# Attention over a convolved sequence: a new order of the first step, a second staging buffer for weights, and batches 3 and 4 split a step later

## The reference, cut to what matters

```python
z   = layer_norm_over_channels(x)
g   = group_norm(z, 32 groups) * gamma + beta
qkv = conv1d(g, w_qkv, 16 taps, "same") + b_qkv        # 256 -> 768 channels
a   = softmax(q k / sqrt(64)) v                        # 4 heads of 64 channels
h   = conv1d(a, w_proj, 5 taps) + b_proj
x1  = x + z + h
t   = layer_norm_over_channels(x1)                     # tokens, 256 wide
out = x1 + t + small table work on t (find first marks, shift, add 2 at the digits)
```

## Time and profile before

| | us |
|---|---|
| median of 3 runs | 1193.16 (1191.77 to 1196.22) |
| the profiled execution | 1190.26 |
| its span on the core | 1188.5 |
| TensorE busy | 1016.5 (86%) |
| VectorE busy | 862.2 (73%) |
| ScalarE busy | 575.1 (48%) |
| GpSimd busy | 231.3 (19%) |

### The profile page before, as it was taken

The page is one execution under the profiler, slowest core; times in us unless marked ns, Lnnn a source line. Parts: engine busy times, 40 slices in busy tenths (PEclk is TensorE's granted clock), DMA queues, the critical chain, the costliest instruction groups (busy, mean ns, idle before and its releaser), DMA issues.

```text
span 1188.5 us, 17778 instructions
## 1 busy us (share of the span) xinstructions
PE 1016.5 (86%) x6760; PEld 670.0 (56%) x6760; DVE 862.2 (73%) x1655; ACT 575.1 (48%) x794; POOL 231.3 (19%) x164
## 2 busy tenths in 40 slices
PE   2737395999999999997989899999999998988854
PEld 1425262666566655664655466656666666756644
DVE  7985976767576578786868566667658675988867
ACT  3443343545445445645547355544435455555522
POOL 2541724100000113112121100000010003223221
PEclk9859697999999999998989899999999999999987
DMA  4240105375275435651654157426533763434412
GB/s 147 80 180 25 45 28 214 74 159 93 50 164 112 80 71 127 145 85 36 195 120 77 36 122 146 89 54 156 95 71 72 191 127 87 107 60 100 107 54 71
DMA packets 279775, 120.44 MB, mean 101 GB/s; under 512 B 267665, under 2 KB 270097, under 8 KB 276753
## 3 DMA queue, kind: packets, MB, share of 16 engines
q1 hardware_dynamic: 279696, 119.37, 43.5%
HBM read 37.43 MB, written 14.81 MB: 44 GB/s over the span
## 4 chain that ended last, share of the span: by engine, by line
PE 45%; DVE 31%; issue 9%; DMA 6%; ACT 5%; POOL 3%; SPq 1%; DVEq 0%; ACTq 0%; POOLq 0%
PE cP L838 11%; PE cM L838 10%; PE cQ L838 8%; PE psV L905 8%; DVE arena L1218 4%; DVE smx L1228 4%; DMA arena<-arena 3%; PE psS L865 3%; PE psT L865 3%; DMA H<-w_qkv 2%; DVE W L1012 2%; DVE W L1005 2%; POOL wsum L466 2%; ACT arena L709 1%; DVE arena L1026 1%
## 5 line engine op out<-in xcount | busy, mean ns | idle before, releaser
L838 PE MATMUL cM<-U,W 128*128 128x256 f16 (+1 forms) x1536 | 230.3, 307 | 47.8 <-ACT m_sb L693 17.8
L838 PE MATMUL cP<-U,W 128*128 128x256 f16 (+1 forms) x1536 | 227.5, 305 | 17.0 <-DVE yqk L1066 11.9
L709 ACT ACTIVATE arena<-arena,smx 128x1024 f16<-128x1024 f32 x128 | 146.8, 1147 | 173.2 <-DVE smx L1261 170.9
L838 PE MATMUL cQ<-U,W 128*128 128x256 f16 (+1 forms) x1536 | 220.6, 300 | 0.0
L838 PEld LDWEIGHTS cM<-U,W 128*128 128x128 f16 x1536 | 152.4, 99 | 120.4 <-ACT m_sb L693 18.1
L838 PEld LDWEIGHTS cP<-U,W 128*128 128x128 f16 x1536 | 151.6, 99 | 84.9 <-DVE yqk L1066 12.2
L838 PEld LDWEIGHTS cQ<-U,W 128*128 128x128 f16 x1536 | 149.2, 97 | 65.1 <-issue 1.6
L1218 DVE SCALAR_TENSOR_TENSOR arena<-arena,smx 128x1024 f16<-128x1024 f32 x128 | 167.6, 1309 | 20.0 <-ACT arena L709 19.9
L905 PE MATMUL psV<-arena 128*128 128x512 f16 x512 | 124.0, 398 | 37.4 <-DMA arena<-arena 37.4
L1270 DVE SCALAR_TENSOR_TENSOR arena<-psV,arena 64x512 f32<-64x512 f32 x32 | 22.0, 689 | 152.0 <-ACT arena L716 151.9
L687 ACT ACTIVATE arena<-psS,smx,esc 128x1024 f32<-128x1024 f32 x64 | 76.9, 1202 | 75.1 <-DVE smx L1229 75.1
(11 more groups left out here) (196 smaller groups left out, 1235.6 us busy)
## 6 DMA issues: line engine op xcount, KB each, us to landing
U<-kept_u SPq DMA_DIRECT2D x6, 2077.0 KB, 9.9
H<-w_qkv SPq DMA_DIRECT2D x12, 1024.0 KB, 7.6
kept_u<-U SPq DMA_DIRECT2D x2, 2077.0 KB, 10.3
kept_u<-arena SPq DMA_DIRECT2D x2, 2077.0 KB, 6.9
arena<-x_tok SPq DMA_DIRECT2D x8, 512.0 KB, 9.0
W<-x_tok SPq DMA_DIRECT2D x4, 1024.0 KB, 6.1
out_tok<-W SPq DMA_DIRECT2D x3, 1024.0 KB, 4.3
kept_h<-arena SPq DMA_DIRECT2D x4, 514.0 KB, 4.5
```

Source lines behind the costliest of these rows:

```text
L709: a(phl[:, i % 3, 0, :], prob[:, i % 2, :], ACT.Copy, scale=smx[:, i % 2, 4:5]) \
L838: last = mm(out, W[:, j, wl, c, wat + tap, :], U[:, slot, ul, c, at:at + width], start=(c == 0 and tap == 0 and wl + ul == 0), stop=(c == ...
```

## The change

It has seven parts.

1. **A second staging buffer.** Tile 1's weights go to `wst_b` at the arena's end, all others to `wst_a` in a new tensor `staging`, which also holds H1 later. Tile 1's load needs no wait. Loads come in four quarters, in steps 2 and 3 one behind each of four transposes.
2. **Scales from squares.** In place of VectorE's two maxima per tile (L987) ScalarE squares the staged weights, 2048 elements a partition, with a sum read-out (kind `wmax`); VectorE adds the two sums (`wtop`), and `pow2(..., squared=True)` takes a power of two from the root.
3. **A new order of step 0** and of steps 3 and 4 in `EXTRA` and `START`; all extra work now stands at the end of its slot on every engine, and TensorE's `weight_top` comes behind the slot's matmuls.
4. **Batches 2 and 3 (the third and fourth) are split a step later**, in steps 1 and 2, from `eo` kept in memory (`keep_eo`, `load_eo`) and straight into `U`; `aside` is gone. VectorE now makes batch 1's differences too.
5. **VectorE's slot**: the row constant right after the y work and ahead of the q/k low parts.
6. **The key copies** (L1092, L1093) become a DMA between partitions (`copy_k`).
7. **Heads a slot later**, at 6, 10, 14 and at slot 0 of the next step. The loops over steps 1, 2 and 5, 6 are written out.

```diff
+        wst_b = arena[:, edge[-1] - WST:edge[-1]].rearrange("p (c s k o) -> p c s k o", c=CT, s=2, k=PH_TAPS)
+        staging = sb("staging", [P, 2 * EO], F32)
+        H1 = staging[:, 0:NB * HR // 2].bitcast(F16).rearrange("p (l b r w) -> p l b r w", l=2, b=NB, r=2)
+        wst_a = staging[:, 0:WST].rearrange("p (c s k o) -> p c s k o", c=CT, s=2, k=PH_TAPS)
+        eo_b = staging[:, 0:EO].rearrange("p (c r w) -> p c r w", c=CT, r=2)
...
-        def pow2(ch, src, k, scale, inverse):
+        def pow2(ch, src, k, scale, inverse, squared=False):
             v = nc.vector
             ch.step(v.tensor_scalar(inverse, src, 1e-30, None, ALU.max))
-            ch.step(v.tensor_scalar(bits[:, 0:1], inverse.bitcast(I32), 0x7F800000, None, ALU.bitwise_and))
+            if squared:
+                k -= 64
+                ch.step(v.tensor_scalar(bits[:, 0:1], inverse.bitcast(I32), 1, 0x7F800000, ALU.logical_shift_right,
+                                        ALU.bitwise_and))
+            else:
+                ch.step(v.tensor_scalar(bits[:, 0:1], inverse.bitcast(I32), 0x7F800000, None, ALU.bitwise_and))
...
-        WSTAGES = ("wmax0", "wmax1", "wscale", "wsum0", "wsum1", "wsum2", "w00", "w01", "wsum3", "w10", "w11")
+        WSTAGES = ("wmax", "wtop", "wscale", "wsum0", "wsum1", "wsum2", "w00", "w01", "wsum3", "w10", "w11")
...
         EXTRA = {
-            0: table(batch_input(1, 0, 4, 4, 7, 7, 7, 10), tile_weights(1, (1, 1, 2, 2, 2, 2, 2, 2, 2, 2, 2)),
-                     batch_input(2, 6, 10, 10, 13, 13, 13, 14), tile_weights(2, (8, 8, 9, 9, 9, 9, 9, 9, 9, 9, 9)),
-                     batch_input(3, 13, 16, 15, 17, 17, 17, 17), [(4, ("wtop", 1)), (10, ("wtop", 2)), (17, ("ring", 0))]),
-            3: table(tile_weights(3, (1, 3, 4, 4, 5, 6, 8, 8, 9, 10, 10)), tile_weights(4, (12, 14, 15, 15, 16, 17, 17)),
-                     [(4, ("wtop", 3)), (15, ("wtop", 4))]),
-            4: table(list(zip((1, 3, 4, 5), [(kind, 4) for kind in WSTAGES[7:]])),
-                     tile_weights(5, (7, 8, 9, 9, 10, 11, 11, 12, 12, 14, 15)),
-                     [(9, ("wtop", 5)), (16, ("pads", 0))]),
+            0: table(tile_weights(1, 1, 1, 2, 3, 3, 4, 5, 5, 6, 6, 7), batch_input(1, 2, 5, 5, 7, 7, 7),
+                     batch_split(1, 8, 9, 9), tile_weights(2, 8, 8, 9, 10, 10, 11, 12, 12, 13, 13, 14),
+                     batch_input(2, 6, 9, 9, 11, 11, 11), batch_input(3, 12, 14, 14, 16, 16, 16)),
+            1: table(batch_split(2, 3, 5, 7), [(1, ("ring", 0))]),
+            2: table(batch_split(3, 3, 5, 7)),
+            3: table(tile_weights(3, 6, 6, 7, 7, 8, 8, 9, 10, 10, 11, 12), tile_weights(4, 15, 15, 16, 16, 17)),
+            4: table(tile_weights(4, no, no, no, no, no, 1, 1, 2, 3, 4, 5),
+                     tile_weights(5, 8, 8, 9, 9, 10, 10, 11, 11, 12, 13, 14), [(16, ("pads", 0))]),
...
+        START = {"vector": ("ln", "gstat", "wscale", "gn", "wsum0", "first0", "wsum1", "first1", "split0", "wsum2", "split1",
+                            "w00", "w01", "split2", "wsum3", "w10", "w11"),
+                 "scalar": ("ln", "wmax", "wsum0", "gn", "first0", "wsum1", "first1", "phase", "split0", "wsum2", "split1",
+                            "w00", "w01", "split2", "wsum3", "w10", "w11"),
+                 "gpsimd": ("wsum0", "wsum1", "split0", "wsum2", "split1", "split2", "wsum3")}
...
+            def copy_k(k, hd):
+                sp.wait_ge(S["qk_lo"], 2 * (2 * k + hd + 1))
+                sp.dma_start(stack[0:D, hd, 1:3, :].rearrange("p k t -> p (k t)"),
+                             stack[D:P, hd, 1:3, :].rearrange("p k t -> p (k t)")).then_inc(S["qk_done"], 16)
...
                     turn(k, u)
+                    if u == 3:
+                        copy_k(k, 1)
+                    if k == 0 and u == 9:
+                        load_eo(3)
+                        keep_u(2)
+                    if k == 1 and u == 9:
+                        keep_u(3)
+                    if k == 1 and 12 <= u < 16:
+                        if u == 12:
+                            sp.wait_ge(S["ulo_done"], SPLITS * NB)
+                        load_w(3, [u - 12])
+                    if 2 <= k < STEPS - 2 and 4 <= u < 8:
+                        load_u(k + 2, u - 4)
+                    if k == 2 and 11 <= u < 15:
+                        load_w(4, [u - 11])
+                    if k == 3 and u in (5, 6):
+                        load_w(5, [2 * u - 10, 2 * u - 9])
+                    if u == 14 and k < STEPS - 1:
+                        copy_k(k + 1, 0)
...
+                if kind == "wmax":
+                    wait(act, "wam_done", k)
+                    if k >= 3:
+                        act.wait_ge(S["conv_done"], GROUPS * (3 * TILES + j + 1))
+                    for c in range(CT):
+                        weights_in(act, k, c)
+                        a(W[:, j, 0, c, 0:2 * PH_TAPS], wst(k)[:, c].rearrange("p s k o -> p (s k) o"), ACT.Square,
+                          accum_out=am[:, 4 + c:5 + c]).then_inc(S["c_m"], 1)
```

More of the change, by code:

```diff
@@ L532, in add_common @@
                     .then_inc(S["ya_done"], 1)
-            def step(n, more=None):
+            for n in range(STEPS):
                 for i in range(SLOTS):
-                    for entry in EXTRA.get(more, {}).get(i, []):
-                        extra(*entry)
                     if i in (3, 9, 16):
@@ L825, in conv_item @@
                 if (g, c, t) == (0, 1, 0):
[L826 removed]
+                    if n == 0 and j == 0:
                         pe.wait_ge(S["ulo_done"], 1)
@@ L1275, in step @@
+                    if attn and i in (6, 10, 14):
+                        heads(k, i // 4 - 1)
+                    if not conv and i == 17:
+                        heads(k, 3)
+                    for entry in EXTRA.get(n, {}).get(i, []):
+                        extra(*entry)
                     if not conv:
```

446 lines of the change are left out of this document (210 added, 236 removed).

## The result

The changed kernel took **1240.81 us** (median, 1239.1 to 1241.99) beside 1193.81 for the kernel before on the same chip: ratio 1.0392 [1.0368, 1.0416], so 47 us slower where 37 faster was forecast. The profiled execution's span is 1239.9 us, 51.4 more than before.

What follows compares the result with a forecast made beforehand. Quiet steps were taken as TensorE-bound near 108 us, with gains only above that and the last step VectorE's; -10 - 11 - 6 + 1 + 0 - 11 = -37 gave a median of 1156 us, own range 1144 to 1168.

Steps and rivals of the forecast that it cites:

- step 0: First step: maxima become squares, splits move out, order changes; -10 us, bounds -20 and +3, value transposes near 177.
- step 1: Second step: batch 3's split leaves its first 12 us, later splits hide in VectorE's slack; -11 us, bounds -13 and -5.
- steps 3 and 4: Steps making the second half's weights: about 30 us above quiet steps against 38 now, taken as 0, bounds -15 and +15.
- last step: Attention and projection: key copies gone and fewer VectorE waits for products; -11 us, bounds -3 and -17.
- Rival (d): Weight tops in steps 3 and 4: split loads make each of three wait 15 us more; +45, 1201 us; chance 0.04.
- sign of being wrong: Whole kernel: TensorE's waits for tops past 70 us, a table load beside a square, or late transposes in steps 2 to 4.
- Rival (a): Waits only change names: step 0 ends where it did, steps 3 and 4 grow by 10; 1176 us; chance 0.2.
- The end of every step: Last unit: earlier reciprocal and key-copy DMA save 3 us, more than TensorE's 1.64 wait; steps 2, 5, 6, 7 give -6.
- What hides them is that slack: Steps 1 and 2: splits, about 6 us of VectorE each, hide in its 37 us free per step.
- Rival (c): Squares on ScalarE: Square needs another table, three tops pay two loads each, 7.7 us; 1164 us; chance 0.04.
- Gone, 9.2 less: Last step: two key copies of 4.62 us under GpSimd's additions vanish; 6 kept, as the next low half pays.
- It is VectorE's: Last step: VectorE bounds it, busy 148.9 of 186.0 us, so removing its copies and waits should give -11.

Runs made afterwards that it cites:

- extra ahead alone: Changed kernel with extra work, from step 1 on, at the slot's head on ScalarE and GpSimd and behind VectorE's low half: 1211.92 us, ratio 1.0158.
- fastest version: Changed kernel with heads, weights of tiles 3 to 5 and extra work (from step 1) placed as before, splits in slots 4, 5, 5: 1163.78 us.
- splits in other slots: Changed kernel with the splits of batches 2 and 3 in slots 4, 5, 5 in place of 3, 5, 7: 1230.43 us, ratio 1.0322.
- heads back: Changed kernel with the heads' output in slots 5, 9, 13 and 17 again, as before the change: 1219.97 us, ratio 1.0236.
- old order of weights: Changed kernel with tiles 3 to 5 in their former slots, VectorE's maxima, and whole loads for tiles 4 and 5: 1224.62 us, ratio 1.0256.

## Why the prediction was wrong, point by point

| part | forecast | measured |
|---|---|---|
| step 0 | -10 | -7.3 |
| step 1 | -11 | -1.3 |
| step 2 | -0.5 | +13.0 |
| steps 3 and 4 | 0 | +40.9 |
| steps 5 to 7 | -4.5 | +1.4 |
| last step | -11 | +4.8 |
| sum | -37 | +51.4 (terms rounded) |

**Steps 3 and 4 are where it failed, and the step that failed is the one not taken.** The text reckoned 30 us above two quiet steps, for the tops' stalls, two slots packed with sums and the slow clock behind them, against 38 in the kernel before, and took 0 as the difference. Measured are 79 above two quiet steps. The change lists that all extra work moves to the end of its slot, and the sum gave that edit no term. Alone it is worth 28.9 us (extra ahead alone), and it is not a matter of busy time: ScalarE's part used to fill the time in which it waits for the maximum, and VectorE's the time in which it waits for the exponential. Put last on both engines, the two halves of one weights tile follow one another and stand between two units. The tops, which were costed, came out at 6.90, 11.22 and 9.72 against 7.6, 4 to 7 and 5 to 7.5. The middle one had its last quarter load late by 3.93 us and the two squares behind it; while VectorE waited for them (7.72 us) the low half of its unit waited too. Rival (d), the only one that made the kernel slower, wanted 15 us more at each top. They came out at most 4.2 above the reckoning, and whole loads with old slots gave 16.2 us, not 45. The text's own sign of being wrong, waits for tops past 70 us in all, did not fire either: they were 66.1 in a kernel 47 us slower. Rival (a) had the direction, steps 3 and 4 longer, but with 10 us and for the tops alone.

**The end of every step: the mechanism was right, the sum was eaten.** "The reciprocal stands ahead of the q/k remainder and the copies go to a DMA": in the kernel before those two edits brought the quiet steps to 107.4, to a tenth what was forecast. Steps 2, 5, 6 and 7 gained 8.6 where 6 was forecast, and steps 3 and 4 another 12 where the text had none, 22 us in all in the medians. The text read the 37.4 us of the earlier trace rows as the last product of a step; by the timeline 16.6 of them lie in the last step and 11.4 in steps 3 and 4, and only the 1.64 of step 2 was carried to the other quiet steps. In the changed kernel the heads took much of it back. The text moved "heads a slot later" only in the last step and kept 5 us for it as a gain; in the other steps it stands just ahead of the last unit of a group, and the move costs 20.8.

**Step 1 and step 2.** "What hides them is that slack" was wrong. VectorE has 37 us free in a step, but the splits stand in the in-order chain of a unit. The value transposes of step 1, forecast near 287, came at 300.7. Even in the fastest version steps 1 and 2 take 117.4 and 114.3, together 231.7 against 231.3 before: spreading two splits over two steps moved 5 us from one to the other and gained nothing there. Their slots in the changed kernel add 8.8 in these steps on top (splits in other slots).

**Step 0** stands: both long tops and the value transposes came within 3 us of the walk (58, 116 and 180), and the 17.8 us stall is gone. How much of the 7.3 is the second buffer, the order or the split moved out isn't shown: no run takes them apart. VectorE lost 31.5 us of work there (145.99 to 114.54) for a step 7.3 shorter. The squares are at the lower end of the estimate of 4.2 to 4.5, by the groups by line and shape of the changed kernel:

```profile
L663 ACT ACTIVATE W<-staging 128x2048 f16<-128x2048 f32 x10 | 19.0, 1903 | 7.1 <-DMA staging<-w_qkv 7.1
...
L663 ACT ACTIVATION_READ_ACCUMULATOR W<-staging 128x1 f32 x10 | 1.9, 193 | 0.0
```

A pair is 4.2 by these means and 3.9 in the timeline of tile 1's (53.73 to 57.60). Rival (c) is refuted: the table loads of the changed kernel stand on L605 (three) and L742 (two), none on L663, by the same view. (Its sentence "none around copies" misread the kernel before, where two more loads stand on L678, the copies of the values.)

**The last step.** "Gone, 9.2 less" took the copies' 4.62 us as their own. GpSimd's two additions, in the kernel before (timeline; the second copy is in the earlier trace rows):

```profile
1033.75 4.89 POOL L508 TENSOR_TENSOR W<-W 128x2048 f32<-128x2048 f32 x1 [28.85 <-ACT W L655]
...
1034.30 4.62 DVE L1092 COPY arena<-arena 64x1024 f16<-64x1024 f16 x1
...
1038.72 4.58 POOL L510 TENSOR_TENSOR W<-W 128x2048 f32<-128x2048 f32 x1
```

and in the changed kernel:

```profile
1084.10 4.52 POOL L551 TENSOR_TENSOR W<-W 128x2048 f32<-128x2048 f32 x1 [31.62 <-ACT W L699]
...
1084.79 4.92 DVE L1259 SCALAR_TENSOR_TENSOR arena<-arena,smx 128x1024 f16<-128x1024 f32 x1
...
1088.70 5.38 POOL L553 TENSOR_TENSOR W<-W 128x2048 f32<-128x2048 f32 x1
...
1092.50 2.67 DVE L1259 SCALAR_TENSOR_TENSOR arena<-arena,smx 128x1024 f16<-128x1024 f32 x1
```

In the version with the copies back, the low half pays again and one copy too, while the other takes 0.42 (timeline):

```profile
1093.65 4.92 DVE L1265 SCALAR_TENSOR_TENSOR arena<-arena,smx 128x1024 f16<-128x1024 f32 x1
...
1098.86 4.35 DVE L1134 COPY arena<-arena 64x1024 f16<-64x1024 f16 x1
1103.14 0.42 DVE L1135 COPY arena<-arena 64x1024 f16<-64x1024 f16 x1
```

So the time is that of the additions, paid by whatever VectorE instruction from buffer to buffer meets them, and more than half of it came back: the two copies' 9.2 us are gone, and the low halves of the last step take 5.5 us more than before, four of them 4.92, 2.67, 2.62 and 3.77 where 1.28 is usual, against one of 4.47 before. The text had this ("the next low half then meets the addition") and kept 6, which is more than the 3.7 that this exchange left. The rule it set beside the sum, from the Trainium skill, "SBUF — State Buffer", section "SBUF: two separate sides", that the pair of ports is held for a whole instruction, is what these rows show: 4.92 us beside an addition of 4.52, 0.42 with none. But the rest of the term failed as well: with the copies back VectorE is 3 us busier in low halves and copies, and the step is no longer (191.1 against 190.8). "It is VectorE's", then, does not hold for every microsecond of VectorE there. What lengthened the last step by 4.8 is partly the heads again: with them back it takes 186.3. In the fastest version, heads back too, it takes 190.6, and step 7 and the last step together 299.9 against 297.5 before; why the last step does not gain stays open.

**The parts together.** Extra work ahead, heads back and the splits in other slots give 55.7 of the changed kernel's time in one version (60.1 by their single runs), the old order of weights 21.3 more (16.2 alone). With all four the change is 28.9 us faster than before, near the 37 forecast, but by other terms, so the nearness is luck: the row constants and the key DMA carry 22 in the kernel before, step 0 some 8.

## What to carry to other kernels

In a kernel like this one, whose engines walk in-order queues, ask of each piece of side work not which engine has free time but what that engine waits for at that place: side work belongs where the engine would stand idle anyway (behind the low half, ahead of the exponential), never between the last result of one unit and the first of the next. An edit that only changes the place in a slot needs its own term in the sum; here it was worth 29 to 36 us. A chain of several engines (a head's output here) belongs behind the work that a product waits for, not ahead of it: 20.8 us. And what a VectorE instruction loses beside a GpSimd one need not go away with the instruction: here more than half of it passed to the next ones. Add up what a wait costs where it reaches the busiest engine, since 86 to 175 us more of waiting on ScalarE stood beside 47 us of time.

## What the runs showed of the hardware that was not expected

A copy of 64x1024 between partitions took 0.42 us with GpSimd still and 4.35 to 4.62 under additions of 4.58 to 5.37. Two differences of 128x1038 took 5.21 us where GpSimd had an addition and a low half of 2.22 and 3.17 at the same time, and 2.39 a slot later. A DMA of 256 KB from buffer to buffer (median 3.9 us to landing), put into the queue ahead of a step's last transpose, cost the transposes nothing that a quiet step shows: with it and the row constants ahead, steps 2, 5 and 6 of the kernel before took 107.4 us with no wait of TensorE.
